# Recurrent attention of a two-layer kernel: keys times values in four column tiles, and a state kept 66 columns wide

## The chip, the core and the metric

The kernel runs on one NeuronCore of a Trainium2 chip. The metric is the device time of one execution in microseconds (us); lower is better. A core has five engines with an instruction queue each: PE (TensorE, matrix products into the accumulation memory PSUM; PEld is its weight load), DVE (VectorE), ACT (ScalarE), POOL (GpSimd) and SP (SyncE, which here issues DMAs). Each queue is worked off in order; engines wait for each other through semaphores.

## What is computed

The reference is a block of two layers on an input of 4 batches, 512 positions and 256 features. Layer 0 adds a recurrent attention (mLSTM, with its own gated MLP) and a mixture-of-experts feed-forward to its input, layer 1 a second attention and a sparsified MLP. The change lies in the recurrent attention of layer 0 alone:

```python
def _mlstm_parallel(q, k, v, i_pre, f_pre):
    B, Hn, S, dqk = q.shape                     # 4, 8 heads, 512, 16
    logfg = jax.nn.log_sigmoid(f_pre)
    Fcum = jnp.cumsum(logfg, axis=-1)
    Dmat = Fcum[..., :, None] - Fcum[..., None, :] + i_pre[..., None, :]
    causal = jnp.tril(jnp.ones((S, S), dtype=bool))
    Dmat = jnp.where(causal, Dmat, -jnp.inf)
    m = jnp.max(Dmat, axis=-1, keepdims=True)
    Smat = jnp.exp(Dmat - m)
    qk = jnp.einsum('bhsd,bhtd->bhst', q, k) / jnp.sqrt(jnp.float32(dqk))
    C = qk * Smat
    n = jnp.maximum(jnp.abs(jnp.sum(C, axis=-1, keepdims=True)), jnp.exp(-m))
    h = jnp.einsum('bhst,bhtd->bhsd', C / n, v) # v has 32 features a head
    return h
```

## The kernel before

The recurrent attention is worked in chunks: each batch b of 4 has C = 4 chunks c of 128 positions. Within a chunk the scores are formed and weighted directly. What earlier chunks contribute goes through a **state**: the sum of keys times values of all chunks before, each decayed. The values have a column of ones appended to each head, so a head has V1 = 33 columns and all 8 heads VW = 264. The keys of 8 heads times 16 features are 128 columns. The product of one chunk's keys (`ktil`, 128 positions by 128) with its values (`v1`, 128 by 264) is a 128 x 264 block of which only the diagonal blocks are wanted (head h's 16 rows with head h's 33 columns); the rest is zeroed by `head_mask`, because the state is used as one full 128 x 264 operand afterwards.

The names that matter, all inside `mlstm_phase`:

- `score(n)` (line 485): four matmuls of two heads each, on 32 rows of the array each ("row tiles"), into banks 0 to 3.
- `turn_k(b)` (line 414): four transposes of the next batch's keys, on the full array.
- `local_state(b, c)` (line 500), for c = 0, 1, 2: one fp32 matmul of 128 x 264, keys times values, into `local_bank` (bank 5). In the trace an fp32 matmul is two weight loads and two matmuls.
- `weighted(b, c)` (lines 511 and 516): eight matmuls of 128 x 33, one a head, and for c > 0 one of 128 x 264, query times state, all into `n_bank` (bank 4).
- `carry(b, c)` on DVE (lines 971 to 984): for c = 0 the masked block is written to `state` (line 977); for c > 0 the masked block goes to `part` (line 980), then, once `weighted(b, c)` has read the old state, `state = state * dexp + part` (line 983).
- `weigh_scores` (line 969), `norm` (line 1026), `sum_squares` (lines 1004 to 1009) on DVE; `weights` (line 701), `evict` (lines 708, 709), `copy_values` (line 684), `copy_keys` (line 679), `high_h` (line 722) on ACT; `mask_weights` (line 839, an affine select) and `inverse_root` (line 853) on POOL.

Order is written out by hand, one list of calls per engine. PE's list for a batch in the middle is: project keys and queries, `score`, `turn_k`, `local_state(b, 0)`, `weighted(b, 0)`, projections, `turn_h`, `score`, `local_state(b, 1)`, `weighted(b, 1)`, projections, `score`, `local_state(b, 2)`, `weighted(b, 2)`, projections, `turn_h`, `score`, `weighted(b, 3)`, output projection. In the last batch there are no projections of a next batch in between. `local_state(b, c)` waits, for c = 1, until `carry(b, 0)` has written `state`, for c = 2 until `carry(b, 1)` has written `part` (both mean that the bank has been read). The layer's dense parts (fused phase, layer 1) follow; they begin at about 136 us and fill the rest of the span.

## Time and profile before

| | |
|---|---|
| device time, median of 3 runs | 704.68 us (704.48 to 705.83) |
| span of the profiled execution, first to last instruction | 703.9 us |
| PE busy | 684.1 us, 97% of the span |
| DVE busy | 516.5 us, 73% |
| ACT busy | 372.7 us, 53% |
| POOL busy | 131.7 us, 19% |
| mean granted TensorE clock | 0.993 |

The three times are of whole executions; the profiled one has a span of 703.9 us, and what lies around the span (start and end of an execution) is about 0.8 us against the median. "Busy" of PE is modelled: matmuls are pipelined, and an engine that is busy need not be at its peak. A row of the timeline gives the start of a group of equal instructions, the time from the first start to the last end, engine, line, operation and tile; brackets give the idle time before it and what ended it. The chain of waits is the list of work that ended last, followed back from the last instruction.

### The profile page before, as it was taken

Reading aid. Unit: us, or ns where it says so; the run is one execution under the profiler, and the core shown is the slowest. Engines: PE = TensorE matmul, PEld = TensorE weight load, DVE = VectorE, ACT = ScalarE, POOL = GpSimd, SP = SyncE. Lnnn points to the kernel's source line nnn. Section 1 sums busy time; section 2 is a strip of 40 time slices with the busy share of each in tenths; the row PEclk is TensorE's granted clock in tenths of the full one; section 3 lists DMA queues with packets and bytes.
Section 4 is the critical chain, followed back from the end, with each engine's and each line's share of the span. In section 5 each row is a group of like instructions: output and inputs, shape, how many; then the busy total and the mean of one; then the engine's idle time right before and its main releaser. Section 6 shows DMA issues by size and latency. Waiting matters only on the chain.

```text
span 703.9 us, 10617 instructions
## 1 busy us (share of the span) xinstructions
PE 684.1 (97%) x4040; PEld 581.4 (83%) x4040; DVE 516.5 (73%) x919; ACT 372.7 (53%) x775; POOL 131.7 (19%) x125
## 2 busy tenths in 40 slices
PE   7999999999999999999999999999999999999997
PEld 7878988878777788887888878887777898889886
DVE  7736567886965757557675576657679998989996
ACT  5886776855735425444253442446566455354541
POOL 7144444510000020000200002000123213203220
PEclk8999999999999999999999999999999999999999
DMA  5087443000100000110001100060000000000000
GB/s 194 5 258 245 127 150 99 0 1 1 62 1 30 1 1 8 54 31 1 1 2 61 31 0 1 7 265 1 1 1 0 1 2 31 1 31 1 1 31 31
DMA packets 24002, 31.17 MB, mean 44 GB/s; under 512 B 1232, under 2 KB 19952, under 8 KB 23184
## 3 DMA queue, kind: packets, MB, share of 16 engines
q1 hardware_dynamic: 23296, 29.18, 12.8%
q10 hardware_dynamic: 656, 1.31, 0.5%
q8 instruction: 32, 0.52, 0.3%
q14 instruction: 18, 0.15, 0.1%
HBM read 28.18 MB, written 2.31 MB: 43 GB/s over the span
## 4 chain that ended last, share of the span: by engine, by line
PE 72%; DVE 18%; ACT 5%; issue 2%; POOL 1%; DMA 1%; DVEq 0%
PE bank L89 21%; PE bank L91 20%; PE bank L90 20%; PE bank L511 4%; DVE l_ring_lo L2533 3%; DVE l_ge L2514 2%; DVE l_h L2529 2%; DVE l_o L2537 1%; PE bank L485 1%; DVE h_raw L1212 1%; DVE l_h L2486 1%; PE bank L500 1%; PE bank L516 1%; DVE h_ring_lo L1217 1%; DVE l_oT_lo L2543 1%
## 5 line engine op out<-in xcount | busy, mean ns | idle before, releaser
L1212 DVE TENSOR_TENSOR h_raw<-h_s,bank 128x512 f32<-128x512 f32 x104 | 71.4, 687 | 107.8 <-ACT h_s L1202 93.5
L1202 ACT ACTIVATE h_s<-bank 128x512 f32<-128x512 f32 x104 | 62.3, 599 | 164.0 <-PE bank L91 162.7
L1217 DVE TENSOR_TENSOR h_ring_lo<-h_raw,h_ring_hi 128x512 fp32r<-128x512 f32 x92 | 68.9, 749 | 0.1
L1206 ACT ACTIVATE h_ring_hi<-h_raw 128x512 fp32r<-128x512 f32 x104 | 64.9, 624 | 2.3 <-DVE h_raw L1212 2.3
L90 PE MATMUL bank<-fused_lo,h_ring_hi 128*128 128x256 f32 x208 | 58.4, 281 | 0.0
L2233 ACT ACTIVATE l_s<-bank 128x512 f32<-128x512 f32 x32 | 19.2, 599 | 64.5 <-PE bank L91 64.5
L89 PE MATMUL bank<-l_xT_hi,l_wgu 128*128 128x512 f32 x128 | 51.3, 401 | 0.1
L89 PE MATMUL bank<-f_yT_hi,mlp_hi 128*128 128x512 f32 x128 | 50.6, 395 | 0.0
L90 PE MATMUL bank<-l_xT_lo,l_wgu 128*128 128x512 f32 x128 | 50.3, 393 | 0.0
L91 PE MATMUL bank<-l_xT_hi,l_lo 128*128 128x512 f32 x128 | 50.2, 393 | 0.0
L91 PE MATMUL bank<-f_yT_hi,fused_lo 128*128 128x512 f32 x128 | 50.0, 390 | 0.0
L90 PE MATMUL bank<-f_yT_lo,mlp_hi 128*128 128x512 f32 x128 | 49.9, 390 | 0.0
L89 PE MATMUL bank<-f_xT_hi,ffn_hi 128*128 128x512 f32 x104 | 41.5, 399 | 0.5 <-DVE h_raw L1212 0.5
L91 PE MATMUL bank<-f_xT_hi,fused_lo 128*128 128x512 f32 x104 | 40.7, 391 | 0.0
L90 PE MATMUL bank<-f_xT_lo,ffn_hi 128*128 128x512 f32 x104 | 40.6, 390 | 0.0
L90 PEld LDWEIGHTS bank<-fused_lo,h_ring_hi 128*128 128x128 f32 x208 | 39.2, 189 | 1.4
L701 ACT ACTIVATE m_W<-m_W,m_tg 128x128 f32<-128x128 f32 x128 | 39.1, 398 | 1.0 <-POOL m_W L839 1.0
L1714 POOL TENSOR_TENSOR late_rstd<-f_vv,minus_half 128x4 f32<-128x4 f32 x3 | 3.0, 1009 | 187.6 <-DVE f_vv L1863 187.6
L89 PE MATMUL bank<-l_wd,l_ring_hi 128*128 128x256 f32 x128 | 36.4, 284 | 1.5 <-DVE l_ring_lo L2533 1.5
L89 PE MATMUL bank<-mlp_hi,h_ring_hi 128*128 128x256 f32 x128 | 35.9, 281 | 1.1 <-DVE h_ring_lo L1217 1.1
L91 PE MATMUL bank<-l_wd,l_ring_lo 128*128 128x256 f32 x128 | 36.2, 283 | 0.0
L90 PE MATMUL bank<-l_lo,l_ring_hi 128*128 128x256 f32 x128 | 36.2, 283 | 0.0
(372 smaller groups left out, 2013.4 us busy)
## 6 DMA issues: line engine op xcount, KB each, us to landing
m_W<-m_scratch SPq DMA_DIRECT2D x16, 512.0 KB, 6.7
fused_raw<-in_fused SPq DMA_DIRECT2D x1, 3584.0 KB, 11.9
res<-in_x SPq DMA_DIRECT2D x4, 512.0 KB, 6.2
fused_raw<-in_fused SPq DMA_DIRECT2D x2, 1024.0 KB, 8.7
f_mask<-expert_weights SPq DMA_DIRECT2D x8, 256.0 KB
l_raw<-in_layer SPq DMA_DIRECT2D x1, 2048.0 KB, 8.6
out_x<-res SPq DMA_DIRECT2D x16, 128.0 KB, 1.9
f_xw<-in_turned_x SPq DMA_DIRECT2D x3, 512.0 KB, 5.9
```

Source lines behind the costliest of these rows:

```text
L89: nc.tensor.matmul(out, w[0], x[0], start=start, stop=False, skip_group_check=True)
L90: nc.tensor.matmul(out, w[0], x[1], start=False, stop=False, skip_group_check=True)
L91: return nc.tensor.matmul(out, w[1], x[0], start=False, stop=stop, skip_group_check=True)
L511: last = nc.tensor.matmul(n_bank[:, h * V1:(h + 1) * V1], W[n % RING][:, h, :], v1[b % 2][:, c, h * V1:(h + 1) * V1], start=h == 0, stop=c ...
L701: last = nc.scalar.activation(w[:, h, :], w[:, h, :], ACT.Exp, bias=tg[:, c, b * H + h:b * H + h + 1], scale=-1.0)
L1202: self.nc.scalar.activation(self.s[u % 2][r, :], gate[r, :], ACT.Silu).then_inc(self.silu.sem, 1)
L1206: self.nc.scalar.activation(self.unit(i, u)[0], self.product(i, u), ACT.Copy).then_inc(self.hi.sem, 1)
L1212: self.nc.vector.tensor_tensor(out=self.product(i, u), in0=self.s[u % 2][r, :], in1=up[r, :], op=ALU.mult).then_inc(self.hidden.sem, 1)
L1217: self.nc.vector.tensor_tensor(out=lo, in0=self.product(i, u), in1=f32(hi), op=ALU.subtract).then_inc(self.lo.sem, 1)
L2233: nc.scalar.activation(sb[u % 2][:, :], gate(u)[:, :], ACT.Silu).then_inc(silu.sem, 1)
L2514: nc.vector.tensor_tensor(out=ge[:, at:at + n, :], in0=ab[:, x, :].unsqueeze(1).to_broadcast([P, n, S]), in1=ab[:, x + 1:GP, :], op=ALU.is ...
L2533: nc.vector.tensor_tensor(out=ring[j][1][:, :], in0=h[c][j][:, :], in1=f32(ring[j][0][:, :]), op=ALU.subtract).then_inc(lo.sem, 1)
```

## The change

Two heads have 32 rows of keys and PW = 66 columns of values. Instead of one 128 x 264 product, `local_state` makes four matmuls, one for each pair of heads: 32 key columns by 66 value columns, each written to its own 32 partitions of the bank (a "column tile" of the array). The result is 128 x 66, with two wanted blocks of 16 x 33 in each 32 rows and two unwanted ones. DVE keeps this narrow state in a new tile `own` (128 x 66): for c = 0 it is copied from the bank, for c > 0 `own = own * dexp + bank`. A second operation then writes the 128 x 264 `state` from it: `own` repeated four times, times `head_mask`. `part` is gone. The semaphore counts move with it: `part_ready` is now given by each write of `own` (three a batch instead of two), and PE's waits for a free bank, and of `turn_h` in the last batch, go by it. For c > 0 the operation on `own` needs no wait for `weighted`; the write of `state` still has that wait, and for c = 0 the copy comes ahead of it.

```diff
+    PW = 2 * V1
...
-    state, part = m("m_state", [P, VW]), m("m_part", [P, VW])
+    state, own = m("m_state", [P, VW]), m("m_own", [P, PW])
...
-    part_ready, state_ready, evicted = sg("m_part", C - 2), sg("m_state", C - 1), sg("m_evicted", 2 * C)
+    part_ready, state_ready, evicted = sg("m_part", C - 1), sg("m_state", C - 1), sg("m_evicted", 2 * C)
...
+    quarters = [slice(r, r + P // 4) for r in range(0, P, P // 4)]
...
                 if b:
-                    pe.wait_ge(state_ready.sem, state_ready.at(b - 1, C - 1))
+                    pe.wait_ge(part_ready.sem, part_ready.at(b - 1, C - 1))
                 else:
                     pe.wait_ge(qt_in.sem, qt_in.at(0, 1))
-            elif c == 1:
-                pe.wait_ge(state_ready.sem, state_ready.at(b, 1))
             else:
-                pe.wait_ge(part_ready.sem, part_ready.at(b, c - 1))
-            nc.tensor.matmul(local_bank[:, 0:VW], ktil[b % 2][:, c, :], v1[b % 2][:, c, :], start=True, stop=True).then_inc(local.sem, 1)
+                pe.wait_ge(part_ready.sem, part_ready.at(b, c))
+            for r, some in enumerate(quarters):
+                last = nc.tensor.matmul(local_bank[some, 0:PW], ktil[b % 2][:, c, some], v1[b % 2][:, c, r * PW:(r + 1) * PW], start=True, stop=True)
+            last.then_inc(local.sem, 1)
...
         def carry(b, c):
             dve.wait_ge(local.sem, local.at(b, c + 1))
-            src, mask = per_head(local_bank[:, 0:VW]), expand(head_mask[:, :], V1)
+            if b or c:
+                dve.wait_ge(state_ready.sem, state_ready.at(b, c))
             if c == 0:
-                if b:
-                    dve.wait_ge(intra.sem, intra.at(b - 1, C))
-                nc.vector.tensor_tensor(out=per_head(state[:, :]), in0=src, in1=mask, op=ALU.mult).then_inc(state_ready.sem, 1)
-                return
-            dve.wait_ge(state_ready.sem, state_ready.at(b, c))
-            nc.vector.tensor_tensor(out=per_head(part[:, :]), in0=src, in1=mask, op=ALU.mult).then_inc(part_ready.sem, 1)
-            dve.wait_ge(part_ready.sem, part_ready.at(b, c))
-            dve.wait_ge(intra.sem, intra.at(b, c + 1))
-            nc.vector.scalar_tensor_tensor(out=state[:, :], in0=state[:, :], scalar=dexp[:, b, c - 1:c], in1=part[:, :],
-                                           op0=ALU.mult, op1=ALU.add).then_inc(state_ready.sem, 1)
+                nc.vector.tensor_copy(own[:, :], local_bank[:, 0:PW]).then_inc(part_ready.sem, 1)
+            else:
+                nc.vector.scalar_tensor_tensor(out=own[:, :], in0=own[:, :], scalar=dexp[:, b, c - 1:c], in1=local_bank[:, 0:PW],
+                                               op0=ALU.mult, op1=ALU.add).then_inc(part_ready.sem, 1)
+            dve.wait_ge(part_ready.sem, part_ready.at(b, c + 1))
+            if c:
+                dve.wait_ge(intra.sem, intra.at(b, c + 1))
+            elif b:
+                dve.wait_ge(intra.sem, intra.at(b - 1, C))
+            nc.vector.tensor_tensor(out=state[:, :].rearrange("p (r h e) -> p r h e", r=H // 2, h=2),
+                                    in0=own[:, :].rearrange("p (h e) -> p h e", h=2).unsqueeze(1).to_broadcast([P, H // 2, 2, V1]),
+                                    in1=expand(head_mask[:, :].rearrange("p (r h) -> p r h", h=2), V1), op=ALU.mult).then_inc(state_ready.sem, 1)
```

No other instruction moves against its neighbours. On PE, in the first batch from the score of chunk 1 on (`m_ktil` are the scaled keys, `m_v` the values with the ones, `m_W` the weighted scores), there stood before:

```order
L485 MATMUL bank<-m_q_102,m_kT_104 128x256 x4
L414 MATMUL bank<-ident,m_kT_105 128x128 x4
L500 MATMUL bank<-m_v_131,m_ktil_129 128x264
L511 MATMUL bank<-m_v_131,m_W_141 128x33 x8
L89 MATMUL bank<-wp_hi,m_yT_hi 128x256
...
L485 MATMUL bank<-m_q_102,m_kT_104 128x256 x4
L500 MATMUL bank<-m_v_131,m_ktil_129 128x264
L511 MATMUL bank<-m_v_131,m_W_142 128x33 x8
```

and now:

```order
L487 MATMUL bank<-m_q_102,m_kT_104 128x256 x4
L416 MATMUL bank<-ident,m_kT_105 128x128 x4
L501 MATMUL bank<-m_v_131,m_ktil_129 32x66 x4
L513 MATMUL bank<-m_v_131,m_W_141 128x33 x8
L89 MATMUL bank<-wp_hi,m_yT_hi 128x256
...
L487 MATMUL bank<-m_q_102,m_kT_104 128x256 x4
L501 MATMUL bank<-m_v_131,m_ktil_129 32x66 x4
L513 MATMUL bank<-m_v_131,m_W_142 128x33 x8
```

One full-array matmul has become four of 32 x 66, in the same place: for c = 0 behind the transposes, for c = 1 and 2 behind the row tiles of the scores. On DVE, in the first batch from the scores' weighting of chunk 1 on, there stood before:

```order
L969 TENSOR_TENSOR m_W_142<-bank,m_W_142 128x1024
L977 TENSOR_TENSOR m_state<-bank,head_mask 128x264
L969 TENSOR_TENSOR m_W_143<-bank,m_W_143 128x1024
L980 TENSOR_TENSOR m_part<-bank,head_mask 128x264
L983 SCALAR_TENSOR_TENSOR m_state<-m_state,m_dexp,m_part 128x264
L991 SCALAR_TENSOR_TENSOR m_den_152<-m_tot 128x16
```

and now:

```order
L971 TENSOR_TENSOR m_W_142<-bank,m_W_142 128x1024
L978 COPY m_own<-bank 128x66
L987 TENSOR_TENSOR m_state<-m_own,head_mask 128x264
L971 TENSOR_TENSOR m_W_143<-bank,m_W_143 128x1024
L980 SCALAR_TENSOR_TENSOR m_own<-m_own,m_dexp,bank 128x66
L987 TENSOR_TENSOR m_state<-m_own,head_mask 128x264
L996 SCALAR_TENSOR_TENSOR m_den_152<-m_tot 128x16
```

For c = 0 one operation of 264 columns has become one of 66 and one of 264; for c > 0 two of 264 have become one of 66 and one of 264.

## Rows read from the trace of the kernel before

**Rows 1.** The page: busy time by engine; chain of waits by engine.
```profile
PE 684.1 (97%) x4040; PEld 581.4 (83%) x4040; DVE 516.5 (73%) x919; ACT 372.7 (53%) x775; POOL 131.7 (19%) x125
...
PE 72%; DVE 18%; ACT 5%; issue 2%; POOL 1%; DMA 1%; DVEq 0%
```

**Rows 2.** Windows: stretch, length, busy time of each engine, PE clock, DMA.
```profile
57.00:125.50 68.50, 68.50 (x552) 60.11 (x550) 44.99 (x89) 49.42 (x150) 33.09 (x19) 1.00 0.44 133
125.50:141.00 15.50, 14.32 (x105) 12.29 (x104) 13.67 (x37) 12.76 (x32) 7.96 (x5) 1.00 0.00 0
```

**Rows 3.** Chain of waits, batch 1, chunks 2 and 3: start, us, what.
```profile
83.67 0.65 PE bank L485 x8
84.31 0.64 PE bank L500 x2
84.95 1.71 PE bank L511 x16
...
89.04 0.64 PE bank L485 x8
89.69 1.90 PE bank L511 x16
```

**Rows 4.** Chain of waits, batch 1, chunk 0, where transposes stand before L500.
```profile
70.53 0.64 PE bank L485 x8
71.17 0.59 PE bank L414 x4
71.76 0.45 PE bank L500 x2
72.21 1.71 PE bank L511 x16
```

**Rows 5.** Weight loads by line: ns min/median/max, first and last start, form.
```profile
L511 PEld LDWEIGHTS bank<-m_v,m_W x256: 186/192/192, 46.4 to 135.1; 128*128 128x128 f32 x128
...
L414 PEld LDWEIGHTS bank<-ident,m_kT x16: 138/140/143, 30.6 to 97.2; 128*128 128x128 f32 x16
...
L451 PEld LDWEIGHTS bank<-ident,roots x1: 97/97/97, 31.1 to 31.1; 128*32 128x32 f32 x1
```

**Rows 6.** Scores on row tiles: all L485, and its first four at 50.18.
```profile
L485 PE MATMUL bank<-m_q,m_kT x128: 374/426/611, 42.1 to 126.1; 32*128 32x256 f32 x128
...
50.18 0.50 PE L485 MATMUL bank<-m_q,m_kT 32*128 32x256 f32 x4
```

**Rows 7.** DVE's operations of the state, and one of 16 columns: ns min/median/max.
```profile
L977 DVE TENSOR_TENSOR m_state<-bank,head_mask x4: 419/423/425, 49.7 to 121.4; 128x264 f32<-128x264 f32 x4
...
L980 DVE TENSOR_TENSOR m_part<-bank,head_mask x8: 421/425/426, 52.1 to 131.0; 128x264 f32<-128x264 f32 x8
...
L983 DVE SCALAR_TENSOR_TENSOR m_state<-m_state,m_dexp,m_part x8: 492/494/1147, 54.1 to 131.5; 128x264 f32<-128x264 f32 x8
...
L991 DVE SCALAR_TENSOR_TENSOR m_den<-m_tot x9: 167/178/195, 54.8 to 136.7; 128x16 f32<-128x16 f32 x7, 128x8 f32<-128x8 f32 x2
```

**Rows 8.** Timeline, last batch: start, us, instruction, idle before and its releaser.
```profile
115.78 0.88 DVE L1033 SCALAR_TENSOR_TENSOR m_hT_lo<-bank,cols,m_hT_hi 128x256 fp32r<-128x256 f32 x2 [0.87 <-ACT m_hT_hi L722]
...
125.73 0.69 DVE L1026 TENSOR_TENSOR m_hh<-m_hh,m_den 128x512 f32<-128x512 f32 x1 [1.53 <-POOL m_den L853]
...
126.82 0.71 PE L500 MATMUL bank<-m_v,m_ktil 128*128 128x264 f32 x2 [0.39 <-DVE m_part L980]
```

**Rows 9.** Timeline, first batch: ACT, and PE's L511 of chunk 1.
```profile
47.91 0.60 ACT L679 ACTIVATE m_ktok<-bank 128x512 f32<-128x512 f32 x1
...
51.00 0.38 ACT L709 ACTIVATE m_sq<-bank 128x256 f32<-128x256 f32 x1
...
51.53 1.94 PE L511 MATMUL bank<-m_v,m_W 128*128 128x33 f32 x16
```

**Rows 10.** Timeline, batches 1 and 2: POOL's affine select, and DVE's slack.
```profile
87.77 1.09 POOL L839 TENSOR_SCALAR_AFFINE_SELECT m_W<-m_W 128x1024 f32<-128x1024 f32 x1 [0.88 <-DVE m_hh L1026]
...
102.66 0.88 DVE L1033 SCALAR_TENSOR_TENSOR m_hT_lo<-bank,cols,m_hT_hi 128x256 fp32r<-128x256 f32 x2 [2.33 <-ACT m_hT_hi L722]
```

More of the change, by code:

```diff
@@ L534, in turn_h @@
             elif f == 1:
-                pe.wait_ge(part_ready.sem, part_ready.at(b, C - 2))
+                pe.wait_ge(part_ready.sem, part_ready.at(b, C - 1))
             else:
```

## The prediction

> **What bounds the kernel now.** I read the page first. PE is busy 97% of the span, DVE 73%, and the chain of waits runs over PE for 72% and over DVE for 18% [rows 1]. These are means over the whole program, and the change touches only the recurrent attention, which runs from about 42 to 136 us, so I then asked for windows of that stage. From 57.0 to 125.5 us PE is busy for all 68.5 us at the full clock (1.00, the 2.4 GHz level), while DVE has 45 us of work and ACT 49 [rows 2]. So in most of the stage the queue of PE alone sets the pace, and a nanosecond taken from or added to PE there moves what follows. From 125.5 to 141 us PE has 1.2 us without work and DVE 13.7 us of 15.5: there DVE has its say [rows 2].
>
> The third view is the chain of waits at the place of the change. It says what `local_state` costs on PE, which is not the length of its rows (they overlap) but the time by which the next group is put off. After the row tiles of the scores, L500 takes 0.64 us and the L511 behind it 1.71; in chunk 3, where there is no L500, L511 itself takes 1.90 behind the scores [rows 3]. So whoever comes first after row tiles pays 1.90 - 1.71 = 0.19 us for the change of tiling, and L500 itself is 0.64 - 0.19 = 0.45. Chunk 0 says the same: L500 stands behind transposes on the full array, and takes 0.45 [rows 4]. 0.45 us for two passes of 264 columns is 0.225 a pass, or 0.056 us for a pass of 66 columns.
>
> **PE, step by step.** Removed are 12 products of 264 columns, added 48 of 66, and, what the diff does not say, a second change of tiling: the scores run on row tiles, the new products on column tiles, `weighted` on the full array. Three terms:
>
> (a) The change into column tiles. Into the full array it costs 0.19 us. Part of this is a weight load that nothing hides: L511 takes 1.71 / 16 = 0.107 us a pass though its 33 columns need only 0.028, so 0.107 is the pace of loading 128 weight columns [rows 3]. The new load has 32 columns. In duration a load of 32 columns took 97 ns against 140 for the like transpose load of 128 [rows 5], 0.04 less; by pure proportion it would be three quarters of 0.107 less, 0.08. So the change costs 0.11 to 0.15; no row shows it, and I take 0.13. If it costs 0.19 like the other, every term below is 0.06 worse a place.
>
> (b) The four products. Nearest is the score, four matmuls on four row tiles: the first four start so close together that all four are done within 0.50 us while one takes 0.478 [rows 6], 0.02 us for three steps, and the whole score of eight passes takes 0.64 with its change of tiling [rows 3], where eight passes of 256 columns in turn would need 8 x 0.218 = 1.75. If column tiles run side by side like that, four products take 2 x 0.056 + 0.02 = 0.13 us. The other bound is that they run in turn: 8 x 0.056 = 0.45, the same as before. No trace here has column tiles; I take the score's row as the nearest, since it is the same data type in the same stage, also four tiles. The difference that could spoil it: the row tiles read different partitions for their weights and data, the column tiles all read all 128.
>
> (c) The change back to the full array, 0.19 us, paid by the L511 behind it (1.90 instead of 1.71) [rows 3].
>
> Sum by place: behind scores 0.13 + 0.13 + 0.19 = 0.45 instead of 0.64, **-0.19 us**. Behind transposes (chunk 0 of batches 0 to 2) there was no change of tiling before, so 0.45 stands against 0.45: **0**.
>
> Not all 12 places count. In batch 0, chunk 0 is followed by a projection that waits for ACT's copy of the keys (47.91 us, 0.60), and in chunk 1 L511 takes 1.94 instead of 1.71 because ACT's eviction at 51.00 frees its bank late [rows 9]: a gain at either is swallowed. In the last batch, PE arrives early at the L500 of chunk 2 and waits for DVE's `m_part` until 126.82 [rows 8], so what chunks 0 and 1 of that batch gain only lengthens the wait. That wait itself moves along with gains made before it: DVE's work leading to it starts at 115.78, released by ACT's copy of PE's transposes [rows 8]. Left are six places behind scores (batch 0 chunk 2; batches 1 and 2, chunks 1 and 2; batch 3 chunk 2) and two behind transposes: 6 x -0.19 + 2 x 0 = **-1.14 us**.
>
> **DVE, step by step.** An operation of 264 columns takes 423 to 425 ns, or 493 with the scalar; one of 16 columns with a scalar 178 [rows 7]. One of 66 is between these two: (425 - 178) / 248 = 1.0 ns a column, so 0.23 us. For c > 0, 0.425 + 0.493 becomes 0.23 + 0.425, 0.26 us less, eight times; for c = 0 the copy comes on top, 0.17 to 0.26 us more with its semaphore, four times. From 57 to 125.5 us DVE has 23 us to spare [rows 2], and this is worth nothing. It counts where PE waits for DVE, at 126.82. The way there runs over DVE and POOL: carry of chunk 0, the small operations, POOL's inverse root, L1026 at 125.73 [rows 8], and then the first operation of the carry of chunk 1, which frees the bank. The first carry makes it 0.26 later, the second (0.23 instead of 0.425) 0.19 earlier: **+0.07 us**.
>
> One risk is moved rather than added. L983 took 1147 ns instead of 494 at worst [rows 7], beside an affine select of POOL that began at 87.77 just before it [rows 10]: an operation with both inputs in SBUF was held up. The new write of `state` has both inputs in SBUF too, in chunk 0 also, where the old one read the bank. If it is held there by 1 us, DVE's next work is L1033, which had 2.33 us of idle time before it [rows 10]. That covers it; without the cover it would cost 1 us a batch in two batches, and the end of the range allows it.
>
> The other edits cost nothing: the renamed waits fall on the same event (the bank has been read), and the wait of `own` on `state_ready` is on DVE's own earlier instruction.
>
> **Sum.** -1.14 + 0.07 = -1.07 us. The span of 703.9 lies 0.8 under the median, and nothing outside the span changes, so 704.68 - 1.07 = **703.6 us**.
>
> **Rivals.**
>
> *Side by side only in part.* If the second pass of a tile must follow its first and only the next tile's first pass goes beside it, there are five steps, 0.28 us: 0.13 + 0.28 + 0.19 = 0.60, so -0.04 behind scores and +0.15 behind transposes, 6 x -0.04 + 2 x 0.15 + 0.07 = +0.1. If the eight loads run in turn, each a quarter of 0.107, and only the last matmul shows, it is 0.08 (the change without its load) + 0.21 + 0.06 + 0.19 = 0.54: -0.6 + 0.2 + 0.07 = -0.35. Time: **704.3 to 704.8**. For it: all four tiles want weights over all 128 partitions, unlike the scores. Against it: nothing that the trace shows.
>
> *In turn (the other side).* The column tiles do not overlap at all; the place is every `local_state`, the price 0.13 + 0.45 + 0.19 = 0.77: +0.13 behind scores, +0.32 behind transposes, 6 x 0.13 + 2 x 0.32 + 0.07 = +1.5, and some +0.1 from batch 0 chunk 0: **706.2**; 706.7 if the change into column tiles costs 0.19. It is slower than before as soon as the four products take over 0.30 us. For it: the work streamed over the array is the same 4 x 66 = 264 columns. Against it: the score's 0.64.
>
> *Loads that wait for running matmuls.* Each pass then pays its load and its columns, 0.027 + 0.056; eight make 0.66, with 0.08 and 0.19 it is 0.93: +0.29 behind scores, +0.48 behind transposes, 1.74 + 0.96 + 0.2 + 0.07 = +3.0, **707.7**. Against it: L511's passes all use the same rows of the array, and a pass costs 0.107, not 0.107 + 0.028; 16 would take 2.16 us, and the row has 1.71 [rows 3].
> By this rule (the Trainium skill, "TensorE: Matmul & The Clock Gate", Part 3, The mechanism) a weight load overlaps running matmuls only when its row group differs, and all four column tiles share theirs; the trace disagrees on the full array (1.71 us where it would give 2.16).
> The same page (Measured speedup vs the span model) reports 2.38x for three column tiles of 512 columns; no run here shows that, and by it the sum would stay at about -1.1.
>
> **How the numbers follow.** Side by side as in the score: 0.48, with its own range 703.0 to 704.2 (terms (a) and (b) by 0.1 at eight places). In part: 0.24. In turn: 0.18. Loads that wait: 0.05. The rest, 0.05, is split between a DVE hold-up that shows and gains at places that I counted as swallowed. The range for 8 in 10 leaves out the loads that wait and the worst of "in turn" above, and a little below: 702.9 to 706.6. About 0.2% (1.4 us) is what a measurement can tell from no change, so faster means under 703.3 and slower over 706.1. Faster: the better third of the first case and swallowed gains that show, 0.20. Slower: most of "in turn", the loads, and part of the rest, 0.24. Within: 0.56.
>
> **What would show it.** In the trace after: (1) the four products' eight matmuls start within some 0.1 us of each other at one `local_state`; if their starts are 0.056 apart, they run in turn; 0.083, the loads wait. (2) In the chain, the column products behind scores at some 0.26 and L511 behind them at 1.90, not 1.71. (3) The copy and the narrow update on DVE at 0.2 us, `state` at 0.42, and one or two of these near 1.1 beside POOL. (4) PE without idle time from 57 to about 124 us, and still waiting for DVE at the last batch's chunk 2. What would make the forecast wrong: a change into column tiles that costs more than 0.19, a load of 32 columns that is no shorter than one of 128 (8 x 0.107), or a swallowed place that is none.

## The result: 0.3% slower

On one chip, in turn, the changed kernel took 706.66 us (median of 20 executions) and the kernel before 704.77 (20): ratio 1.0031, interval 1.0016 to 1.0046. Ratios here and below come with a 95% interval and are not the quotients of the medians shown; they leave out the executions over 1.5% above the fastest of their kernel (714.46 us in e1, 714.58 in e3, and 2353 in e4, which the table leaves out too). The forecast was 703.6, with a range that ended at 706.6. It missed by the sign: a small gain was forecast, and a loss of 1.9 us came. Single executions of the changed kernel lie between 703.67 and 714.18 us, and the profiled one is the 703.67, so its trace shows the kernel at its best and not at its median.

Its page, the parts that answer to [rows 1], has PE's busy time 3.2 us lower and DVE's 1.7 higher:

```profile
PE 680.9 (97%) x4112; PEld 577.1 (82%) x4112; DVE 518.2 (74%) x923; ACT 372.3 (53%) x775; POOL 131.6 (19%) x125
...
PE 70%; DVE 20%; ACT 5%; issue 2%; POOL 1%; DMA 1%; SPq 0%; DVEq 0%
```

The chain of waits of the changed kernel in batch 1 (start, us, what), chunks 0, 2 and 3, answers to [rows 3, 4]. L487 are the scores, L416 the transposes, L501 the new products, L513 `weighted`:

```profile
70.13 0.59 PE bank L416 x4
70.72 0.25 PE bank L501 x8
70.97 1.90 PE bank L513 x16
...
82.44 0.64 PE bank L487 x8
83.08 0.25 PE bank L501 x8
83.34 1.90 PE bank L513 x16
...
87.62 0.64 PE bank L487 x8
88.27 1.90 PE bank L513 x16
```

Behind scores, L501 and L513 take 0.25 + 1.90 = 2.15 us where L500 and L511 took 0.64 + 1.71 = 2.35: -0.20 a place. Behind transposes it is 2.15 against 0.45 + 1.71 = 2.16: nothing. These are the forecast's -0.19 and 0.

DVE's three operations of the state (count, ns min/median/max, first and last start) answer to [rows 7]:

```profile
L987 DVE TENSOR_TENSOR m_state<-m_own,head_mask x12: 432/434/1353, 49.1 to 129.5; 128x264 f32<-128x264 f32 x12
L980 DVE SCALAR_TENSOR_TENSOR m_own<-m_own,m_dexp,bank x8: 274/276/278, 51.3 to 129.2; 128x66 f32<-128x66 f32 x8
L978 DVE COPY m_own<-bank x4: 217/219/221, 48.9 to 119.6; 128x66 f32<-128x66 f32 x4
```

In windows of the stage (columns as in [rows 2]) PE has no idle time up to 123.5 us and waits 0.89 us in the next window; the clock stands at 1.00 throughout:

```profile
57.00:117.30 60.30, 60.30 (x533) 52.56 (x532) 41.71 (x83) 44.53 (x135) 29.26 (x18) 1.00 0.47 143
117.30:123.50 6.20, 6.20 (x68) 4.89 (x66) 5.11 (x11) 4.80 (x17) 2.64 (x1) 1.00 0.00 0
123.50:126.00 2.50, 1.61 (x24) 1.11 (x23) 1.80 (x4) 2.29 (x9) 0.63 (x1) 1.00 0.00 0
126.00:140.00 14.00, 13.21 (x94) 11.74 (x93) 12.16 (x36) 11.42 (x28) 7.55 (x4) 1.00 0.01 1
```

PE's timeline of the last batch (start, us, instruction, idle before and its releaser) shows that wait, as the last of [rows 8] did for the kernel before, with the scores that open the batch (117.38) and chunk 2 (123.51); the `weighted` of chunks 1 and 3 are for comparison below:

```profile
117.38 0.71 PE L487 MATMUL bank<-m_q,m_kT 32*128 32x256 f32 x8
118.02 0.32 PE L501 MATMUL bank<-m_v,m_ktil 128*32 128x66 f32 x8
...
121.10 1.95 PE L513 MATMUL bank<-m_v,m_W 128*128 128x33 f32 x16
122.88 0.69 PE L518 MATMUL bank<-m_state,m_qt 128*128 128x264 f32 x2
123.51 0.71 PE L487 MATMUL bank<-m_q,m_kT 32*128 32x256 f32 x8
...
125.11 0.32 PE L501 MATMUL bank<-m_v,m_ktil 128*32 128x66 f32 x8 [0.89 <-DVE m_own L980]
...
127.56 0.69 PE L518 MATMUL bank<-m_state,m_qt 128*128 128x264 f32 x2
...
133.29 0.69 PE L518 MATMUL bank<-m_state,m_qt 128*128 128x264 f32 x2
```

The kernel before, at the same places:

```profile
119.21 0.71 PE L485 MATMUL bank<-m_q,m_kT 32*128 32x256 f32 x8
...
125.72 0.71 PE L485 MATMUL bank<-m_q,m_kT 32*128 32x256 f32 x8
...
129.51 0.69 PE L516 MATMUL bank<-m_state,m_qt 128*128 128x264 f32 x2
```

All eight matmuls of a `local_state` lie within 0.32 us, and one of them takes 0.233 by median, so they start within 0.1 us of each other: they do run side by side. The two traces laid beside each other give the sum. At the first scores of batch 1, PE is 0.84 us earlier (56.97 against 57.81); that is from the start-up, where the trace of before has the clock at 0.50 from 11.6 to 18.5 and 38.9 to 42.4 us and that of after only from 37.9 to 41.3. Take it off, and PE is earlier by 1.0 us at the start of the last batch (117.38 against 119.21), by 0.9 behind the wait (125.11 against 126.82), by 1.1 at the query-times-state product after it (127.56 against 129.51). **At the full clock the change does what was forecast: -1.1 us, against -1.07.** So the profile that the change was judged by cannot hold the loss; the executions that the profiler did not look at do.

### The profile page after: what moved, and what is told of

The parts are those of the page before. It is cut to its first block, busy times and chain, and to the rows that moved or that the text cites. A ratio compares the mean times of both kernels' runs of the same rounds, so it can differ in the third digit from the quotient of the medians.

```text
span 701.8 us, 10768 instructions
## 1 busy us (share of the span) xinstructions
PE 680.9 (97%) x4112; PEld 577.1 (82%) x4112; DVE 518.2 (74%) x923; ACT 372.3 (53%) x775; POOL 131.6 (19%) x125
## 4 chain that ended last, share of the span: by engine, by line
PE 70%; DVE 20%; ACT 5%; issue 2%; POOL 1%; DMA 1%; SPq 0%; DVEq 0%
PE bank L89 21%; PE bank L91 20%; PE bank L90 20%; PE bank L513 3%; DVE l_ring_lo L2538 3%; DVE l_ge L2519 2%; DVE l_h L2534 2%; DVE l_o L2542 1%; DVE h_raw L1217 1%; DVE l_h L2491 1%; DMA res<-in_x 1%; PE bank L487 1%; DVE h_ring_lo L1222 1%; PE bank L518 1%; DVE l_oT_lo L2548 1%
```

## Experiments

Each run gives the time and the mean granted clock of its executions. In the changed kernel they go together: of the 20 executions the one at 0.996 took 703.67 us, those at 0.990 some 706.4, at 0.988 some 707.8, at 0.983 710.6, at 0.976 714.18. The table sorts all runs by what TensorE does in the last batch (ratios against the kernel before on the same chip, with their intervals; "low clock": a mean granted clock of 0.990 or less):

| kernel | executions | median us | over 706 us | low clock | ratio |
| --- | --- | --- | --- | --- | --- |
| before, in four sets | 140 | 704.6 to 704.9 | 32 | 4 | |
| e2 before again | 12 | 704.84 | 4 | 1 | 1.0002 [0.9985, 1.0020] |
| changed, first runs | 20 | 706.66 | 15 | 14 | 1.0031 [1.0016, 1.0046] |
| e1 changed again | 12 | 706.54 | 7 | 6 | 1.0006 [0.9988, 1.0024] |
| e12 changed, third | 12 | 705.11 | 5 | 5 | 1.0002 [0.9985, 1.0018] |
| e3 tiles, DVE as before | 12 | 705.16 | 5 | 4 | 1.0011 [0.9984, 1.0039] |
| e4 wide product, new DVE | 11 | 705.57 | 3 | 0 | 1.0001 [0.9986, 1.0017] |
| e11 tiles in last batch only | 12 | 708.65 | 11 | 9 | 1.0045 [1.0027, 1.0063] |
| e14 the same again | 12 | 708.51 | 10 | 10 | 1.0045 [1.0028, 1.0062] |
| e13 the same, filled | 12 | 705.79 | 5 | 4 | 1.0009 [0.9991, 1.0027] |
| e6 tiles except in last batch | 12 | 704.42 | 5 | 2 | 0.9998 [0.9978, 1.0018] |
| e16 the same, filled | 12 | 704.95 | 5 | 3 | 1.0014 [0.9993, 1.0034] |
| e9, e15 changed, filled | 12, 11 | 705.77, 704.78 | 4, 3 | 1, 3 | 1.0004, 1.0005 |
| e5 changed, wait filled | 12 | 706.28 | 7 | 2 | 1.0012 [0.9995, 1.0030] |
| e10 changed, two waits filled | 12 | 705.05 | 5 | 2 | 1.0005 [0.9987, 1.0023] |
| e7 before, longer wait | 12 | 707.05 | 7 | 1 | 1.0023 [1.0008, 1.0038] |
| e8 before, wait filled | 11 | 705.47 | 3 | 0 | 1.0004 [0.9992, 1.0017] |

(The kernel before beside the first runs, 20 executions without a clock on record, had 3 over 706.) Counts out of 12 are rough, and the same kernel differs from set to set, each on another chip: the changed one has 5 to 7 of 12 and 15 of 20 over 706, and in e1 and e12 the interval of its ratio reaches over 1. A loss clear of noise came in the first runs alone; over all three sets, 27 of 44 executions of the changed kernel are over 706 and 32 of 140 of the kernel before. What follows rests on counts that lie far apart.

Neither count tells where in an execution the clock fell. The line at 0.990 lies just under what one long fall leaves: e2's traced execution (708.15 us, 10.2 us at half clock) has a mean of 0.993. At 0.993 or less are 49 of 140 executions of before and 35 of 44 of the changed kernel. Falls that begin ahead of the first changed instruction (about 45 us) count too: e4's traced execution (707.57 us) has its one long fall from 37.4 to 47.7 us, and e1's has 10.2 of its 17.1 us at half clock ahead of 46 us.

### First question: clock, DVE, or the scatter of a run?

The theories were C (TensorE's clock falls more often), D (DVE's new operations cost) and S (the start-up differs from execution to execution). e1 and e2 are the two kernels as they are, for further executions and traces.

> The changed kernel as it is, for the clock and span of more executions and a second trace. Theory C (clock): PE is some 1.1 us shorter wherever it runs at 2.4 GHz, but most executions fall to the 1.2 GHz level once or more after 42 us: time 705 to 709, mean clock 0.985 to 0.993, and if the traced execution is such a one, a stretch at 0.5 shows between 46 and 140 us. Rival S (start): the differences between executions lie before 42 us alone; after 42 us every trace is at 1.00. Rival D (DVE): time varies with the write of the state held up beside POOL, and not with the clock.

> The kernel before as it is, timed as the others are. Theory C: mean clock 0.992 to 0.996 in nearly all executions, time 704.2 to 705.5, half the scatter of the changed kernel. Rival S: the same scatter of clocks and times as the changed kernel, and the same mean at the same clock but for 1.1 us.

e3 has the column tiles alone; DVE makes its 264-column operations, reading the 66 columns four times over:

```diff
-            nc.tensor.matmul(local_bank[:, 0:VW], ktil[b % 2][:, c, :], v1[b % 2][:, c, :], start=True, stop=True).then_inc(local.sem, 1)
+            for r, some in enumerate(quarters):
+                last = nc.tensor.matmul(local_bank[some, 0:PW], ktil[b % 2][:, c, some], v1[b % 2][:, c, r * PW:(r + 1) * PW], start=True, stop=True)
+            last.then_inc(local.sem, 1)
...
-            src, mask = per_head(local_bank[:, 0:VW]), expand(head_mask[:, :], V1)
+            src = local_bank[:, 0:PW].rearrange("p (h e) -> p h e", h=2).unsqueeze(1).to_broadcast([P, H // 2, 2, V1])
```

> The change on PE alone: four column tiles, while DVE works as before on 264 columns (it reads the 66 columns of the bank four times under the mask). Theory C: as slow and as scattered as the changed kernel, 705 to 709, clock 0.985 to 0.993, with the wait of the last batch's chunk 2 at about 126.8 less 1.7 us. Rival D: like the kernel before less 1.1 us, about 703.6, clock above 0.992.

e4 has DVE's new operations alone, behind the one wide product, so every pair of heads gets the first pair's state:

```diff
-            for r, some in enumerate(quarters):
-                last = nc.tensor.matmul(local_bank[some, 0:PW], ktil[b % 2][:, c, some], v1[b % 2][:, c, r * PW:(r + 1) * PW], start=True, stop=True)
-            last.then_inc(local.sem, 1)
+            nc.tensor.matmul(local_bank[:, 0:VW], ktil[b % 2][:, c, :], v1[b % 2][:, c, :], start=True, stop=True).then_inc(local.sem, 1)
```

> The change on DVE alone: one product of 264 columns as before, DVE's narrow operations read its first 66 columns (so the state is that of the first two heads in every place, and the result is not the reference's). Theory C: like the kernel before, 704.5 to 705, clock above 0.992. Rival D: 706 to 707, scattered like the changed kernel. By the terms of the prediction alone +0.07 us.

The changed kernel was over 706 us in 7 more of 12 executions, some of the others at 703.66 and 704.3; by medians it was 1.7 us above the kernel before, though the interval of the ratio reaches over 1. The kernel before did not show the small scatter that C expected: four of 12 in e2 lie at 707.4 to 708.2. With tiles alone (e3) executions of 0.990 or less stay, up to 714.58; with DVE's part alone (e4) there are none, though six of 11 are at 0.993. That speaks for C and for PE's half of the change, and against D. S is right in part: there are falls at the start in both kernels, but not there alone.

The trace of e1 is of an execution of 706.8 us, and its windows show where its clock fell in the last batch: behind the long wait (0.89 us, ahead of 126.28).

```profile
118.50:128.11 9.61, 8.72 (x99) 6.94 (x97) 7.82 (x17) 8.01 (x29) 3.27 (x1) 1.00 0.00 0
128.11:134.94 6.83, 6.83 (x32) 6.44 (x32) 5.61 (x19) 4.06 (x10) 5.47 (x3) 0.50 0.01 2
```

The kernel before has it too, in the trace of e2 (708.15 us), from 125.81 on, behind its own wait of 0.40 us:

```profile
118.00:125.81 7.81, 7.42 (x65) 5.75 (x64) 6.14 (x13) 5.90 (x22) 3.27 (x1) 1.00 0.01 2
125.81:136.05 10.24, 10.24 (x44) 9.59 (x45) 7.47 (x21) 6.12 (x17) 5.63 (x3) 0.50 0.00 0
```

So the fall to 0.50 (the 1.2 GHz level) in the last batch is no invention of the change. That it comes more often with the change is what the counts suggest; the runs below test it.

### Second question: does the longer wait do it?

Theory W: the wait at the third `local_state` of the last batch has grown, and the clock falls because TensorE stands still there. Theory T: the tiles leave TensorE with too little work over the whole batch, wait or no wait. e5 fills the wait with four idle products of 128 columns, e8 does it in the kernel before; e7 lengthens the wait of the kernel before by one DVE operation (0.55 us); e6 has before's code in the last batch and the change in the other three.

```diff
 e5, e8, ahead of the last batch's third local_state:
+        pe.wait_ge(og_in.sem, og_in.at(B - 1, 2))
+        idle_products(4)
 e7, ahead of the last batch's second carry:
+        nc.vector.tensor_tensor(out=eq[:, 0, :], in0=eq[:, 0, :], in1=eq[:, 1, :], op=ALU.mult)
 e6, in local_state (and in carry the same way):
+            if b == B - 1:
+                nc.tensor.matmul(local_bank[:, 0:VW], ktil[b % 2][:, c, :], v1[b % 2][:, c, :], start=True, stop=True).then_inc(local.sem, 1)
+                return
```

> The changed kernel with four idle products of 128 x 128 (some 0.86 us of fp32) on PE ahead of the last batch's third local_state, where PE waits 0.9 us for DVE. Theory W (the lengthened wait lets PE's clock fall in the last batch): no or few falls there any more, median 703.5 to 704.2, under the kernel before by 0.6 to 1.3 us. Theory T (the narrow tiles themselves, over the whole last batch, show too little work): the falls stay at half of the executions or more, median 705.5 to 707.

> The changed kernel in batches 0 to 2, and the product of 264 columns with the wide carry in the last batch, as before. Both W and T: the last batch is that of before, wait 1.1 us, so falls in a quarter of the executions as before, and the gain of 0.9 us of batches 0 to 2 stays: median 703.7 to 704.1. If the median is 706 or more, the loss does not come from the last batch.

> The kernel before with one more DVE operation (384 columns, some 0.46 us) ahead of the last batch's second carry, so that PE's wait grows from 1.1 to 1.6 us, as in the changed kernel, with no column tiles. W: falls in the last batch in half of the executions or more, median 706 to 708. T: falls in a quarter, median 705.2 (before plus 0.46).

> The kernel before with the four idle products ahead of the last batch's third local_state. PE waits 0.8 us there, so they cost 0 to 0.1. W: the falls of before (about a quarter of its executions, 707.3 to 708.2) vanish, median 704.5 to 704.9, highest under 706. T: they stay.

e7 made the wait as long as the change does (timeline of PE; before it was 0.39):

```profile
126.53 0.71 PE L500 MATMUL bank<-m_v,m_ktil 128*128 128x264 f32 x2 [0.86 <-DVE m_part L980]
```

It brought 7 of 12 executions over 706, where before had 10 of 35 on that chip. This fits W, but counts of this size can differ so by chance. Filling the wait did not take the falls from the changed kernel: in e5's trace the filling stands from 124.14 us to the products at 125.23, no idle time is left, and 7 of 12 executions are over 706, though only 2 at a low clock. W is not the whole of it. e8 leaves it open: its filling takes 1.00 us where the wait of before was 0.39 to 0.40, so it costs time by itself (median 705.47), and one of 11 executions is over 707 where before had 9 of 35. e6 missed what both theories expected (falls in a quarter, median 703.7 to 704.1): 5 of 12 are over 706, two of them at a clock of 0.988, and the median is 704.42.

### Third question: where does the fall start?

e9 puts two idle products behind each of the first two `local_state`s of the last batch, e10 seven into its two waits; e11 has the column tiles in the last batch alone, with DVE as before; e12 is the changed kernel a third time.

```diff
 e9, last batch:
+        pe.wait_ge(og_in.sem, og_in.at(B - 1, 2))
         score(n + 1)
         local_state(b, 0)
+        keep_busy(2)
...
         local_state(b, 1)
+        keep_busy(2)
 e10, ahead of the third local_state, and of project_out(b - 1, 1):
+        keep_busy(4)
...
+        keep_busy(3, 6)
 e11, in e3's local_state:
+            if b < B - 1:
+                nc.tensor.matmul(local_bank[:, 0:VW], ktil[b % 2][:, c, :], v1[b % 2][:, c, :], start=True, stop=True).then_inc(local.sem, 1)
+                return
```

> The changed kernel with four idle 128-column products in the last batch, two behind the first local_state and two behind the second, on a PSUM bank that is free there; nothing else of it differs. Theory W (the clock falls because TensorE stands still for one longer wait at the third local_state): the wait stays about as long (1.4 to 1.6 us), the late falls stay as often as without the filling, about 7 of 12 executions over 706, median 706 to 707. Theory T (the clock falls because the whole stretch of the last batch shows TensorE with less work than before): the filling gives back some 0.3 us of work, the falls become about as rare as in the kernel before (3 of 12 over 706), median 703.9 to 704.8. Both: with the granted clock at 1.00 in the last batch the execution ends at 703.5 to 704.1, since the products lie in time in which TensorE waits.

> The changed kernel with seven idle 128-column products in the last batch, all where TensorE waits: four ahead of the third local_state, three ahead of the second output projection. Theory W: falls at the third local_state go (at most 3 of 12 executions over 706), as they should have done with four products alone, which 7 of 12 contradicted; so W, if it holds, must name a second wait, the one ahead of the output projection, which is filled here too. Theory T: more work in the whole stretch, falls 3 of 12 or fewer. Neither (the fall has nothing to do with how much TensorE works there): 6 to 8 of 12 over 706, median 706 to 707. With the granted clock at 1.00 all through the last batch the execution ends at 703.5 to 704.2.

> The kernel before with the four column tiles in the last batch alone (batches 0 to 2 keep the one wide product; VectorE keeps its 264-column operations throughout, reading the 66 columns four times over in the last batch). At full clock: 704.6 to 705.0, the time of before less the two places of the last batch, whose gain the wait swallows. If the narrow tiles in the last batch are what makes the clock fall there: 5 to 8 of 12 executions over 706, median 705.5 to 707.5, slower than before. If it takes VectorE's changed order, or a last batch that comes earlier, as well: falls as in the kernel before (3 of 12), median 704.7 to 705.2.

> The changed kernel again, beside the other three on the same chip, for more executions and a third trace of it. Theory that its loss is a clock that falls in the last batch more often than before: 6 to 9 of 12 executions over 706, those at a granted clock of 0.996 or more at 703.6 to 704.3, median 706 to 707; a trace whose execution is over 706 shows a stretch at half clock between 122 and 137 us. Theory that the loss belonged to the chips of the earlier runs: 3 of 12 over 706, median 704 to 705.

e11 is the clearest run of the study: three places with column tiles, all in the last batch, and 11 of 12 executions are over 706 (5 to 8 were expected), ratio 1.0045. Tiles at these three places are enough for the loss. That the other nine places do nothing is not shown: e6 and e16, which have tiles there and the wide product in the last batch, have 5 of 24 executions at 0.986 to 0.988, a clock that none of the 140 of before comes down to, and their traces are of others. The counts of the other three runs are less clear. e12 has 5 of 12 over 706 and a median of 705.11, between what its two theories expected; e10's 5 of 12 lies between its theories as well; e9's 4 of 12 is near T's 3, but its median of 705.77 is above T's 704.8, and its traced execution (705.91) has falls ahead of 43 us alone.

The trace of e12 (an execution of 707.75 us) shows a fall with no wait of PE ahead of it; these are its windows:

```profile
57.00:117.00 60.00, 60.00 (x532) 52.23 (x524) 42.35 (x83) 44.35 (x135) 29.16 (x18) 1.00 0.48 141
117.00:122.09 5.09, 5.09 (x62) 4.12 (x60) 4.99 (x11) 3.92 (x15) 1.54 (x1) 1.00 0.00 0
122.09:135.74 13.65, 13.65 (x69) 11.80 (x68) 8.73 (x25) 8.38 (x26) 7.37 (x4) 0.50 0.01 1
```

PE is busy for all of the 65 us ahead of 122.09, and the clock goes from 1.00 to 0.50 while it is busy, in the `weighted` of chunk 1, ahead of the scores of chunk 2 and so of the long wait behind them. PE's timeline of the same run shows the half clock in the durations:

```profile
117.08 0.71 PE L487 MATMUL bank<-m_q,m_kT 32*128 32x256 f32 x8
...
117.97 1.97 PE L513 MATMUL bank<-m_v,m_W 128*128 128x33 f32 x16
...
120.79 2.43 PE L513 MATMUL bank<-m_v,m_W 128*128 128x33 f32 x16
123.04 1.23 PE L518 MATMUL bank<-m_state,m_qt 128*128 128x264 f32 x2
...
125.36 0.45 PE L501 MATMUL bank<-m_v,m_ktil 128*32 128x66 f32 x8
...
137.23 0.69 PE L518 MATMUL bank<-m_state,m_qt 128*128 128x264 f32 x2
```

L518 takes 1.23 us where the profiled execution took 0.69, and at 125.36 no wait is left: PE itself is now late. From the first scores of the last batch to its last L518 it is 137.23 - 117.08 = 20.15 us, against 133.29 - 117.38 = 15.91 at the full clock: 4.2 us more, and the two executions differ by 707.75 - 703.67 = 4.1. **Between these two executions, the loss lies in that stretch.**

The Trainium skill ("TensorE: Matmul & The Clock Gate", Part 1, What's actually happening) says that the gate sets the rate by how busy TensorE has been. Here the profile counts it as busy throughout and the clock falls nonetheless, so busy time in the profile does not tell whether the clock holds.

e10's fall starts in the same place (121.85, ahead of both of its fillings), e3's too (122.34), and e11's at 126.35, its last batch being 4 us later. Measured from the first scores of the last batch, these three falls and e12's start 4.9 to 5.3 us in, and all four kernels have unfilled tiles up to there. The falls of e1, e2 and e7 start 7.7 to 10.5 us in, behind the wait. There are two places, then: one behind a wait, seen with tiles (e1) and without (e2, e7), and one ahead of it, seen only with unfilled tiles. That the wait makes the fall behind it is not shown.

### Fourth question: too little work, or tiles as such?

M: column tiles or the changes of tiling themselves make the clock fall. e13 is e11 with e9's filling, e14 e11 again on the same chip, e15 e9 again, e16 is e6 with one idle product behind each of the first two `local_state`s.

```diff
 e13 against e14, last batch:
+        pe.wait_ge(og_in.sem, og_in.at(B - 1, 2))
         score(n + 1)
         local_state(b, 0)
+        keep_busy(2)
...
         local_state(b, 1)
+        keep_busy(2)
```

> The kernel before with column tiles in the last batch alone, and two idle 128-column products behind each of its first two local_states (0.55 us at each place, in time that the wait at the third had left free). Theory T (the column tiles leave TensorE with too little work in the last batch, whatever it waits for): the stretches at half clock between 122 and 137 us become rare, at most 4 of 12 executions over 706.6 against 9 to 12 for the same kernel without the filling; median 704.6 to 706. Theory M (column tiles as such, or the changes of tiling, make the clock fall): 8 to 12 of 12 over 706.6, median 707.5 to 709. Theory W (the wait at the third local_state): that wait is filled too by the later start, so it expects few as T does; against W speak the traces in which the clock fell at 121.9 to 122.3 us, ahead of that wait, with TensorE busy.

> The same kernel without the filling, on the same chip: 9 to 12 of 12 executions over 706, median 707.5 to 709, if the eleven of e11 were no accident of its chip; 3 to 5 of 12 and 704.5 to 706 if they were. A trace of an execution over 706.6 shows half clock from some point between 121 and 129 us.

> The changed kernel with the same filling, again: by T at most 2 of 12 executions over 706.6 (one in e9), those with the clock low only ahead of 46 us at 705 to 706.5, the rest at 703.6 to 704; median 703.8 to 705.9. If e9 was luck: 5 to 7 of 12 over 706.6, median 706 to 707.

> Column tiles in batches 0 to 2, the wide product and VectorE's wide operations in the last batch, and one idle 128-column product behind each of its first two local_states (0.275 us each, 0.55 in all, of which the wait of 0.37 us at the third takes up the most). At full clock 703.7 to 704.2. By T: at most 2 of 12 over 706.6, median 703.9 to 705, which is below both kernels by 0 to 1 us. If falls have nothing to do with TensorE's work there: 4 to 6 of 12 over 706.6, median 704.5 to 706.

e14 repeats e11: 10 of 12 over 706. With the filling it is 5 of 12, the median goes from 708.51 to 705.79 us, and the intervals of the two ratios do not overlap. The tiles are the same in both. M expected 8 to 12 over 706.6, T at most 4, and e13 has 4: tiles as such do not suffice. (The traced executions of e11 and e14, 710.21 and 710.64 us, have two falls of 10.2 us each, and the first begins ahead of 38 us, where their code is that of before.) The windows of e14 show the early fall, 5.1 us into the last batch with PE never idle in it:

```profile
121.10:126.26 5.16, 5.16 (x63) 4.19 (x61) 4.89 (x10) 4.00 (x15) 1.85 (x1) 1.00 0.02 3
126.26:136.50 10.24, 10.24 (x54) 8.53 (x54) 6.76 (x18) 5.42 (x19) 5.29 (x3) 0.50 0.00 0
```

In those of e13 the early fall is gone and a shorter, late one is left, behind PE's next waits:

```profile
118.90:130.84 11.94, 11.25 (x117) 9.11 (x116) 10.15 (x23) 9.13 (x33) 5.06 (x3) 1.00 0.01 1
130.84:134.26 3.42, 3.42 (x19) 3.42 (x18) 3.32 (x11) 2.52 (x7) 3.42 (x2) 0.50 0.00 0
```

For the changed kernel itself the evidence is weaker. The low-clock executions go from 25 of 44 to 4 of 23 (e9 and e15), but over different chips; on the one chip that had both (e12 and e9) they go from 5 of 12 to 1 of 12, while those over 706 go from 5 to 4 and the median does not fall. e15 has 3 of 11 over 706.6 where T expected at most 2 of 12. e16 has 4 of 12, again over T's 2, as the rival had it by which falls have nothing to do with TensorE's work there. At the full clock the filling costs nothing, since PE's timeline of e9 has the products in the time of the wait, of which nothing is left:

```profile
122.26 0.71 PE L568 MATMUL bank<-ident 128*128 128x128 f32 x4
...
125.85 0.32 PE L501 MATMUL bank<-m_v,m_ktil 128*32 128x66 f32 x8
```

Its fastest executions are at 703.6 to 703.8. But no version is below the kernel before by its interval: e6 and e16 come to ratios of 0.9998 and 1.0014, and e9 and e15 to 1.0004 and 1.0005. Falls elsewhere go on; e15's trace has one from 46.6 to 63.6 us, ahead of any filling and 1.4 us behind the first column tiles of the program (45.16 us).

**What stays open.** The filling adds work for TensorE and also moves what follows by 0.55 us a place; that it is the work and not the moving was not tried apart. What tiles in batches 0 to 2 do to the clock is open too: no trace of a low-clock execution of e6 or e16 was taken. How much of the changed kernel's loss falls to the early place, the late place and the start is not known, since the executions without a trace give only a mean clock. Why tiles in the last batch alone (21 of 24 over 706) are worse than tiles everywhere (27 of 44 in the changed kernel, 5 of 12 in e3) is not known.

## Why the prediction was wrong, point by point

**Terms (a) and (b), 0.13 + 0.13: right.** L501 took 0.25 us for the change into column tiles and four products together, against 0.26 forecast. "Side by side as in the score", the likeliest case, is what happened; "in part", "in turn" and "loads that wait" did not. The last rests on a rule of the Trainium skill ("TensorE: Matmul & The Clock Gate", Part 3, The mechanism); by the prediction's estimate the place would have taken 0.66 + 0.08 = 0.74 us. The trace disagrees.

**Term (c), 0.19 paid by the line behind: right.** L513 took 1.90 in chunks 0, 2 and 3 above, as predicted for L511.

**Which places count: right.** Up to the last batch PE gained 1.0 us (forecast 5 x 0.19 = 0.95), then the two swallowed places only lengthened the wait: from the start of the scores of chunk 2 to its products it grew from 1.10 to 1.60 us. Nothing asked what a longer wait would do besides swallowing a gain; in e7 it cost 2.2 us by median, of which the fastest executions (704.68 to 705.2 at a clock of 0.994 or more) show some 0.4 to be the operation that was added.

**DVE: right in sum.** The copy took 0.22, as forecast; the narrow update 0.276 against 0.23, so 66 columns with a scalar are dearer than the line between 16 and 264 gives. From the start of the last batch to the end of the wait PE gave back 0.1 us, +0.07 forecast. The hold-up of `state` beside POOL came four times at 1.30 to 1.35 us (at 73.34, 86.61, 98.72 and 111.98 us, in batches 1 and 2), where one or two at 1.1 were forecast; PE waited for none of them.

**The step that failed: "The span of 703.9 lies 0.8 under the median, and nothing outside the span changes."** The sum was made at the clock of one execution (1.00 in both windows of [rows 2]) and then set off against a median over executions, as if every execution kept that clock. The two numbers are not of the same execution either. In the execution of 703.67 us the time is 1.9 us longer than the span (701.8), and in the others it is much the same, so a span of 703.9 belongs to a time of some 705.8. By that the profiled execution is the slowest of the three, 705.83, and not the median, and the 0.8 us is not the time around the span. That trace has two falls at the start, and a clock of 0.993. The forecast left out a term: the granted clock in the last batch, and what the change does to it. There the change puts eight passes of 66 columns, side by side in quarters of the array, in the place of two of 264 on the whole array, and fills the time that it saves with nothing, since PE goes on to wait. Executions at a granted clock of 0.990 or less went from 4 of 140 to 25 of 44, those over 706 us from 32 of 140 to 27 of 44. With tiles in the last batch alone, 21 of 24 are over 706 and the ratio is 1.0045 twice. At a clock of 0.996 or more the medians are 703.66 us (5 executions of the changed kernel) and 704.55 (88 of before): the forecast's gain, seen in few executions of the changed kernel.

**The rivals.** The one on the other side ended at 706.2 to 706.7, and the result, 706.66, lies there by chance: its mechanism did not occur. The chance of 0.24 for slower was made up of the wrong cases, all of them products that take longer. What in [rows 2] could have raised it: PE has 1.2 us without work between 125.5 and 141 us, and e2's fall starts there (125.81); but one profiled execution cannot say how often a clock gives way, and the falls with PE busy could not be read from it at all. Two figures of "in turn" are off by its own terms: with the 0.1 of batch 0 its time is 706.3, and the four products make the kernel slower from 0.26 us on (8 x 0.264 = 2.11), not 0.30. Neither moved the forecast.

## What to carry to other kernels

A change that takes work from TensorE where TensorE does not set the pace gains nothing there, and it can cost the clock. Filling such a stretch with idle products gave most of the loss back here (e13 against e14), and leaving the wide products in it kept the time of before (e6); neither came out faster than before. Count the low-clock executions, and take a trace of one. Judge a sub-percent change by the distribution over executions with the clock beside each, since the profiled one may be the best of twenty. When a gain is swallowed by a wait, price the longer wait as well.

## What the runs showed of the hardware beyond that

- The granted clock fell from 1.00 to 0.50 with PE busy throughout the 65 us before (e12), and in e14 with PE busy for all of the 5.16 us before; the matmuls of that stretch were row tiles, column tiles of 66 columns and passes of 33 columns.
- Eight matmuls of 66 columns in four column tiles, all over 128 partitions of weights, put the next group off by 0.25 us with their change of tiling; the weight loads did not make them run in turn.
- The same kernel on the same chip took from 703.66 to 714.46 us (e1), in step with its mean granted clock (0.996 to 0.976).
